# A graph network on one core: where layer 0's compared row lies, and how often GpSimd waits between scatters

## What is computed

```python
x = layernorm(x + segment_sum(x[src], dst))                        # layer 0
msg = relu(x[src] + edge_attr)                                     # layer 1: only its last of 5 sub-layers counts
x = layernorm(x + relu(relu(((1+eps)*x + segment_sum(msg, dst)) @ W1.T + b1) @ W2.T + b2))
x = layernorm(x + segment_sum(x[cols] * edge_weight, rows) @ W)    # layer 2: rows = src, cols = dst
x = layernorm(x + segment_sum(norm * gate * x[src], dst))          # layer 3
```

## Time and profile before

| | |
|---|---|
| median of 3 runs | 11638.95 us (11632.47 to 11648.19) |
| the profiled execution | 11615.17 us, its span 11613.4 us |
| TensorE's mean granted clock | 0.72 |
| busy in the span | PE 52%, PEld 47%, DVE 58%, ACT 35%, POOL 32% |

### The profile page before, as it was taken

How to read it: one execution, slowest core, us unless ns; L and a number is a source line. 1 busy time by engine, 2 the same in 40 slices (tenths; PEclk the granted TensorE clock), 3 DMA queues, 4 the chain that set the end, 5 groups by cost and what they waited for, 6 DMA issues and landing times.

```text
span 11613.4 us, 288892 instructions
## 1 busy us (share of the span) xinstructions
PE 5989.1 (52%) x120824; PEld 5480.6 (47%) x120824; DVE 6785.5 (58%) x8337; ACT 4030.2 (35%) x6116; POOL 3672.4 (32%) x3346
## 2 busy tenths in 40 slices
PE   5777500000000000029976666666666666688886
PEld 5666400000000000028865656666666666688886
DVE  8999700000000000029978888886777777888895
ACT  2333200000000000015535555554888888233331
POOL 6778876676766666650000000000000000000000
PEclk8888755555555555569988888886666676799997
DMA  6554111111111111125536555553555554455552
GB/s 115 95 100 70 34 31 30 29 32 29 31 30 32 30 30 30 29 59 170 170 102 199 191 192 192 192 195 119 187 186 184 186 187 172 131 169 168 169 169 81
DMA packets 1123616, 1319.69 MB, mean 114 GB/s; under 512 B 581317, under 2 KB 869253, under 8 KB 1122183
## 3 DMA queue, kind: packets, MB, share of 16 engines
q1 hardware_dynamic: 716445, 572.55, 19.0%
q10 hardware_dynamic: 302952, 675.90, 17.5%
q0 software_dynamic: 103168, 54.68, 2.2%
HBM read 902.26 MB, written 400.43 MB: 112 GB/s over the span
## 4 chain that ended last, share of the span: by engine, by line
another core or an unknown queue 29%; DVE 23%; ACT 16%; issue 13%; PE 8%; ACTq 4%; DVEq 4%; DMA 3%; SPq 0%
ACT far_now L1322 9%; DVE hot_d L919 8%; ACT near_now L1285 4%; DMA source_marks<-near_now 3%; PE banks L1516 2%; PE banks L1426 2%; DVE hot_r L793 2%; DVE hot_t L929 2%; DVE left L1067 2%; DVE msg_z L1075 2%; ACT msg_z L1314 1%; DVE moved L772 1%; DVEq L796 1%; PE banks L1451 1%
## 5 line engine op out<-in xcount | busy, mean ns | idle before, releaser
L652 POOL DMA_INDIRECT slot_table<-recs,idx_now x3224 | 3611.3, 1120 | 1409.1 <-issue 960.1
L919 DVE TENSOR_TENSOR hot_d<-lodl,banks 128x2560 bf16<-128x2560 bf16 (+1 forms) x884 | 1487.1, 1682 | 1830.8 <-remote 1626.6
L1516 PE MATMUL banks<-hot_d,msg 128*96 128x256 bf16 x10192 | 1624.5, 304 | 1654.7 <-issue 1127.8
L1516 PEld LDWEIGHTS banks<-hot_d,msg 128*96 128x96 bf16 x10192 | 1237.6, 134 | 1803.0 <-issue 1264.5
L1254 ACT CAST msg<-banks 128x480 bf16<-128x480 f32 (+1 forms) x1040 | 522.2, 554 | 4103.2 <-remote 3260.0
L929 DVE TENSOR_SCALAR hot_t<-lo_bc,part_col 128x1280 bf16<-128x1280 bf16 (+1 forms) x884 | 529.1, 599 | 1774.2 <-remote 1379.4
L1525 PE MATMUL banks<-parts,hot_t 128*128 128x96 bf16 x5096 | 330.9, 217 | 2314.6 <-issue 1852.8
L1525 PEld LDWEIGHTS banks<-parts,hot_t 128*128 128x128 bf16 x5096 | 287.2, 103 | 2433.7 <-issue 2417.7
L1322 ACT CAST far_now<-hot_td 128x1792 fp8e4<-128x1792 bf16 x728 | 1187.8, 1679 | 34.3 <-DVE hot_td L937 33.5
L1570 PE MATMUL banks<-x_win,hot_td 128*128 128x32 bf16 x30576 | 881.9, 184 | 210.4 <-issue 193.6
L1570 PEld LDWEIGHTS banks<-x_win,hot_td 128*128 128x128 bf16 x30576 | 837.9, 101 | 227.4 <-issue 213.4
(11 more groups left out here) (183 smaller groups left out, 9748.4 us busy)
## 6 DMA issues: line engine op xcount, KB each, us to landing
lo_bc<-row_table ACTq DMA_DIRECT2D x364, 448.0 KB
dl_bc<-row_table SPq DMA_DIRECT2D x364, 448.0 KB, 4.3
target_marks<-far_now ACTq DMA_DIRECT2D x364, 448.0 KB, 3.5
dl_bc<-target_marks SPq DMA_DIRECT2D x364, 448.0 KB, 4.2
lo_bc<-row_table ACTq DMA_DIRECT2D x468, 320.0 KB
slot_table<-zeros SPq DMA_DIRECT2D x52, 1617.0 KB, 11.6
rec_in<-slot_table ACTq DMA_DIRECT2D x364, 231.0 KB, 2.7
source_marks<-near_now ACTq DMA_DIRECT2D x364, 224.0 KB, 2.3
```

The source lines that it names most:

```text
L652: pool.indirect_dma_start(out=slot_dram[c.number], out_offset=bass.IndirectOffsetOnAxis(ap=idx_now[:, c.slot, g:g + 1], axis=0), in_=recs[ ...
L919: v.tensor_tensor(hot[:, blk.slot, 0:half], ids.unsqueeze(2).to_broadcast([P, half, WIN, 2]), steps.unsqueeze(1).to_broadcast([P, half, WI ...
L1516: mm = t.matmul(banks[0:3 * D, 6 + blk.par, 0:WIN], rows[:, blk.slot, g, :], hot[:, blk.slot, g // 2, :, g % 2], start=(blk.b == 0 and g = ...
```

## The change

Layer 0's `hot_d` compares with `iota_d` in SBUF, as layer 3's does; the copy to PSUM ahead of layer 0, with its drain, goes. Layer 1 keeps its copy and its PSUM row. RUN is 8 in place of 16, so GpSimd waits behind g = 7, 15, 23, 31, 39, 47 and 55: 7 waits in a chunk in place of 3.

```diff
-RUN = 16
+RUN = 8
...
                 ids = lodl[:, bass.ds(blk.chunk, 1), HB + blk.h0:HB + blk.h0 + blk.n].rearrange(
                     "p c (a t) -> p (c a) t", t=2)
-                steps = far_d if q < 2 else iota_d[:, :, :]
+                steps = far_d if q == 1 else iota_d[:, :, :]
                 v.tensor_tensor(hot[:, blk.slot, 0:half], ids.unsqueeze(2).to_broadcast([P, half, WIN, 2]),
...
             def sum_sources():
                 start_sweep(0)
-                v.tensor_copy(banks[:, 5, 0:WIN], words_of(iota_d))
-                dve.drain()
                 first = SourceBlock(0, 0)
```

## The result

The changed kernel took 10207.15 us, median of 4 runs (10194.56 to 10236.65), the kernel before 11643.57 (4 runs) on the same chip: a ratio of 0.877, 95% interval 0.8749 to 0.8792. I had forecast 11265 and a range of 10850 to 12080.

A forecast was written before the change was run, and what follows sets the result against it. GpSimd's scatters set the end up to 5142 us, then the stages behind. 11615 + 347 (waits) + 330 (held scatters) - 840 - 106 (layer 0's rest, node pass) - 104 (layer 1) = 11242, so 11265 on the median's scale; range 10850 to 12080.

The forecast's parts named there:

- Layer 1 ... I expect completions to lag there again: Layer 1 beside the scatters: TensorE's completions lag, 157 us a block, 21 blocks done, 104 us taken off the total.
- VectorE changes instruction at least twice in a block: Layer 0: one scatter let through a block, 517 scatters in 983 us, GpSimd losing 330 us (bounds 0 and 423).
- Rival 2: Layer 1 also runs freely, overtakes the scatters and goes on at their pace: 9830 us, chance 0.15.
- The waits: GpSimd: 208 more landing waits at 1.67 us each move its end out by 347 us (up to 424).
- The row in SBUF: Layer 0's hot_d: same operation time from SBUF as from PSUM (2013 ns each at 3584 elements), so nothing counted.
- The base: Layers 0 and 1: TensorE's completions lag while GpSimd issues scatters unhindered, and not while VectorE holds GpSimd up.

The follow-up runs named there:

- the row alone: The changed kernel with RUN = 16 in place of 8: 11446 us where the kernel before took 11615; 9907 us on chip 14, ratio 1.088.
- RUN 16: The kernel before's setting, unchanged: GpSimd waits behind each 16th scatter, 3 waits a chunk; 9099 us beside the run with one wait a chunk.
- the waits alone: The kernel before with RUN = 8 in place of 16, both rows in PSUM: 10353 us where the kernel before took 11615; 9468 where it took 9099.
- one wait a chunk: The kernel before with one landing wait a chunk, behind the 31st scatter, in place of three: 8829 us where the kernel before took 9099.
- every other block: The changed kernel, but layer 0 compares from PSUM in odd blocks: 9918 us where the kernel before took 11615; 9719 where it took 9099.
- RUN 8: The changed kernel's setting, kept with every other block: GpSimd waits behind each 8th scatter, 7 waits a chunk; 9918 us where the kernel before took 11615.

## Why the prediction was wrong

**"Layer 1 ... I expect completions to lag there again ... 157 us a block, 21 blocks."** This step failed, and it is worth the most. The number was about right for the row alone (117 us a block), wrong for the changed kernel, because I had entered the waits as a cost only. On the late chip they are what keeps layer 1 at 11.5 us a block: 11446 us without them and 10207 with them, 11615 and 10353 with both rows in PSUM. How a wait does that isn't shown. Worth (334 - 21) x 4.91 = 1537 us.

**"VectorE changes instruction at least twice in a block, which lets a scatter through, so I take one a block."** The second failed step, of the other sign. A change of instruction lets nothing through; a real gap of 0.20 us does (466 scatters), and so does an operation with an operand in PSUM (449). One scatter in ten blocks: 62 for 517, a loss of 982 - 62 x 1.27 = 903 us in place of 330. GpSimd's end came 536 us later than I had it (6355 for 5819). With both corrections my sum on the profiled execution's scale is 11242 - 1537 + 536 = 10241; it took 10236.65. The two errors had hidden each other in part.

**Rival 2, "layer 1 runs freely too", at 9830 and a chance of 0.15**, is the nearest in time, but on the late chip not in mechanism. It said that layer 1 overtakes the scatters and goes on at their pace, a chunk behind. There layer 1 never caught up: GpSimd took about 92 us a chunk (2677 instructions of GpSimd at 64 a chunk in 3843 us), layer 1 took 7 x 11.5 = 80.5, started some ten chunks behind and was still 30 blocks behind at the end, held by late completions and never by a chunk's records. On a prompt chip the changed kernel shows just what rival 2 said. An idle time of VectorE in layer 1, first on the late chip, then on the prompt one, and there the largest idle times of two engines:

```profile
3003.34 0.62 DVE L974 TENSOR_TENSOR total<-banks,rec_in 128x448 f32<-128x448 f32 x1 [8.96 <-remote]
```

```profile
3010.92 0.62 DVE L994 TENSOR_TENSOR msg<-left,msg 128x448 bf16<-128x448 f32 x1 [49.48 <-ACT msg L1296]
```

```profile
DVE msg L994 <- ACT msg L1296: 2330.0, 232, 57.6
POOL slot_table L652 <- DMA slot_table<-recs,idx_now: 853.7, 362, 10.2
```

Seven blocks of a chunk pass at 4 to 6 us each, then all wait up to 58 us for the next chunk's records. In all fourteen traces from prompt chips layer 1 has 352 of 364 blocks done when the last scatter ends.

**"The waits": 1.67 us each, 347 in all.** About right for the waits of this change: on prompt chips 208 waits cost 301 us beside the row in SBUF (10208 - 9907) and 369 without it. It is no price for a wait as such: 104 waits fewer than RUN 16 gave 270 us, 2.6 each.

**"The row in SBUF: the operation's own time should not move."** Right: 1481 ns at 2560 elements on the changed kernel's page for 1478. By the page VectorE: DVE Perf Modes of the Trainium skill (The perf-mode tier table) it would have nearly halved; no run here shows it. The Trainium skill (GPSIMD Engine Reference, Specifications) has GpSimd's interfaces shared with VectorE's two-input instructions. These traces agree, and put a price on it: a scatter held for 18.62 us.

**The base.** I had written that the prediction fails in its base "if the lag of TensorE's completions turns out not to follow from unhindered scatters". It does not follow from them alone: on chip 14 scatters go at 1.27 us in layer 0, VectorE's `hot_d` not holding them up, and nothing lags; on three more chips the kernel before takes the same time. There the change does only its two costs: the row alone 9907 - 9105 = 802 us, of which (677 - 62) x 1.27 = 781 are scatters not done in layer 0; the waits alone 369; both together 1103, 68 less than the sum. The waits themselves were shorter beside the row (853.7 us in 362, for 992.2 in 362 with the waits alone); why isn't shown. On the late chip the same costs buy a free layer 0 and a layer 1 at 11.5 us a block. I read one chip's trace as the kernel's nature, which no view of that trace could have told me; the time before on a second chip would have.

What stays open: what differs between the chips, and whether it is the chip or the time; and whether on a late chip a mere gap in GpSimd's issues frees TensorE's completions or only the landing. The nearest other test, a wait for scatters issued some steps earlier, which need not leave a gap, wasn't tried.

No kernel run here beats both on both kinds. On a prompt chip it is one wait a chunk (8829 us), whose time on a late one is not known; on a late chip every other block with RUN 8 (9918), which on a prompt one is 7% slower than the kernel before and 5% faster than the changed one.

## What to carry to other kernels

Where an engine that sets the end shares a path with another one, ask what gap the other leaves: here back-to-back VectorE operations that read SBUF alone stopped GpSimd's scatters for ten blocks at a time, and 0.2 us of pause in each block let one through. A wait on the engine that sets the end can be a gain, as on the late chip; test waits and data placement apart, since here the row freed layer 0 alone and the waits acted on both layers. And where a stretch is idle for "remote" reasons, time the unchanged kernel on a second chip before any change is judged by it.

## What the runs showed of the hardware that was not expected

- The same kernel differs between chips (or between the times at which they ran): the kernel before takes 11615 to 11644 us on one or two and 9099 to 9128 on four. On the late ones TensorE's completions reach ScalarE and VectorE up to 55 us late beside GpSimd's scatters; on chip 14 the same layer takes 1.89 us a block. What makes them late is open.
- On a late chip a landing wait behind each 8th scatter in place of each 16th takes layer 0, with its row in PSUM, from 52 to 4.67 us a block, and layer 1, beside layer 0's row in SBUF, from 117 to 11.5.
- One GpSimd scatter lasts 0.96 us beside a VectorE operation with an operand in PSUM, and 18.62 us beside an unbroken row of operations that read SBUF alone (`hot_t` and `hot_d` of ten blocks).
